# One reciprocal of a product in place of two reciprocals: products moved to GpSimd in a fused attention and neighbour kernel

## The reference, cut to what matters

```python
idx = _knn(x_loc, 30)                       # top 30 of 1024, per point
rel = pts[bidx, idx] - pts[:, :, None, :]   # xr, yr, zr
sxy2 = xr * xr + yr * yr
r2 = sxy2 + zr * zr
rho = jnp.sqrt(jnp.maximum(r2, TINY))
sxy = jnp.sqrt(jnp.maximum(sxy2, TINY))
deg_r, deg_p = r2 < TINY, sxy2 < TINY
theta = jnp.arctan2(jnp.where(deg_r, 0.0, zr), jnp.where(deg_r, 1.0, sxy))
phi = jnp.arctan2(jnp.where(deg_p, 0.0, yr), jnp.where(deg_p, 1.0, xr))
sph = jnp.stack([rho, theta, phi], axis=-1)
feat = jnp.concatenate([sph, sph - jnp.mean(sph, axis=-1, keepdims=True)], axis=-1)
# three layers of matmul, batch norm and leaky relu on feat, then a softmax over the 30
```

## Time and profile before

| what | before |
|---|---|
| median of 3 runs | 6317.76 us (6315.41 to 6318.28) |
| the profiled execution: its time, its span | 6316.55 us, 6314.8 us |
| TensorE matmul busy | 5517.6 us (87%) |
| VectorE busy | 5699.2 us (90%) |
| ScalarE busy | 4499.4 us (71%) |
| GpSimd busy | 3397.5 us (54%) |

### The profile page before, as it was taken

The page is one execution under the profiler, slowest core; times in us unless marked ns, Lnnn a source line. Parts: engine busy times, 40 slices in busy tenths (PEclk is TensorE's granted clock), DMA queues, the critical chain, the costliest instruction groups (busy, mean ns, idle before and its releaser), DMA issues. The chain is left out here.

```text
span 6314.8 us, 227176 instructions
## 1 busy us (share of the span) xinstructions
PE 5517.6 (87%) x82516; PEld 3384.3 (54%) x82516; DVE 5699.2 (90%) x8045; ACT 4499.4 (71%) x17145; POOL 3397.5 (54%) x3375
## 2 busy tenths in 40 slices
PE   7888888888888888888888888888669859999999
PEld 3555555555555555555555555555433347777776
DVE  7999999999999999999999999999855687777786
ACT  7888888888888888888888888888604623333333
POOL 3466666666666666666666666666620033333332
PEclk9999999999999999999999999999879979999999
DMA  2333333333333333333333333333340023333332
GB/s 45 95 105 97 99 98 96 95 95 107 98 110 91 99 98 96 97 97 109 96 107 93 97 97 97 97 108 92 106 108 0 0 64 89 94 87 88 84 94 74
DMA packets 651349, 568.72 MB, mean 90 GB/s; under 512 B 553072, under 2 KB 574832, under 8 KB 616208
## 3 DMA queue, kind: packets, MB, share of 16 engines
q1 hardware_dynamic: 613264, 284.51, 19.2%
q10 hardware_dynamic: 36864, 268.45, 12.0%
HBM read 384.76 MB, written 67.24 MB: 72 GB/s over the span
## 5 line engine op out<-in xcount | busy, mean ns | idle before, releaser
L722 ACT ACTIVATE prob<-SC,row_max 128x64 f32<-128x64 f32 x6144 | 1842.2, 337 | 389.7 <-DVE row_max L1046 381.6
L835 POOL TENSOR_TENSOR prob<-prob,row_rec 128x512 f32<-128x512 f32 x768 | 830.2, 1082 | 1433.5 <-DVE row_rec L1054 1403.5
L722 ACT ACTIVATION_READ_ACCUMULATOR prob<-SC,row_max 128x1 f32 x6144 | 1393.0, 230 | 0.0
L1038 DVE FIND_INDEX8 nbr<-top,dist 128x8 uint16<-128x1024 f32 x1024 | 1234.4, 1217 | 0.0
L1031 DVE MAX8 top<-dist 128x8 f32<-128x1024 f32 x1024 | 1190.8, 1203 | 1.7
L1033 DVE MATCH_REPLACE8 dist<-top,dist 128x1024 f32<-128x1024 f32 x768 | 923.3, 1206 | 0.0
L586 PE MATMUL SC<-k_bd,q_t 128*64 128x256 f32 x6144 | 907.1, 420 | 0.0
L1697 ACT ACTIVATE dense<-DM 128x512 f32<-128x512 f32 x512 | 305.6, 597 | 747.0 <-PE DM L1656 746.7
L607 PEld LDWEIGHTS PT<-ident,prob 128*128 128x128 f32 x3072 | 361.7, 145 | 833.8 <-issue 815.6
L1805 DVE TENSOR_TENSOR d_oh_a<-lo,iota_a 128x4096 bf16<-128x4096 bf16 x256 | 583.9, 2291 | 239.7 <-PE DM L1656 239.1
L607 PE MATMUL PT<-ident,prob 128*128 128x128 f32 x3072 | 490.9, 284 | 351.0 <-ACT prob_t L729 350.3
(11 more groups left out here) (187 smaller groups left out, 9475.7 us busy)
## 6 DMA issues: line engine op xcount, KB each, us to landing
low_all<-low_scratch ACTq DMA_DIRECT2D x256, 1024.0 KB, 5.0
k_bd<-k_t SPq DMA_DIRECT2D x3072, 16.0 KB, 1.9
placed<-compact SPq DMA_DIRECT2D x256, 192.0 KB, 3.8
ctx<-in_ctx SPq DMA_DIRECT2D x32, 512.0 KB, 6.2
mask<-in_mask SPq DMA_DIRECT2D x32, 512.0 KB, 8.7
xb<-in_x SPq DMA_DIRECT2D x32, 512.0 KB, 3.3
x_scratch<-xb SPq DMA_DIRECT2D x32, 512.0 KB, 6.9
y_scratch<-y_b SPq DMA_DIRECT2D x32, 512.0 KB, 6.6
```

Source lines behind the costliest of these rows:

```text
L722: last = act.activation(prob[:, s % 4, g * CHUNK:(g + 1) * CHUNK], SC[:, s % 2, g * CHUNK:(g + 1) * CHUNK], ACT.Exp, bias=row_max[:, s % 2 ...
L835: pool.tensor_tensor(pr, pr, row_rec[:, r % 2, :].unsqueeze(2).to_broadcast([128, 8, CHUNK]), ALU.mult).then_inc(normed, 1)
L1038: last = dve.max_index(nbr[:, uu % BPB, t, k * 8:(k + 1) * 8], best, row)
```

## The change

The two denominators are multiplied on GpSimd to one product `both` (128x256) directly behind `base`. VectorE takes the reciprocal of that product alone, half as many values. While it does, GpSimd multiplies each leg by the other angle's denominator (two instructions of 128x256 at step 43, with a wait for their end), and `ratio` becomes that cross product times the one reciprocal, read for both angles. Apart from this, the two clamps at step 36 use one operation each (`max`, `is_ge`) without the multiplication by 1.0.

```diff
 APART_AT, SQUARE_REL_AT, R2_AT, ROOT_AT, LEGS_AT, ACROSS_AT, BASE_AT, INVERSE_AT = 34, 35, 36, 38, 39, 41, 42, 43
+CROSS_AT = 43
...
-        hot, ratio, base = low_all, apart[:, 0:2, :], sqr[:, 0:2, :]
+        hot, ratio, base, both = low_all, apart[:, 0:2, :], sqr[:, 0:2, :], sqr[:, 2, :]
...
                     pool.tensor_tensor(base[:, :, :], sides[:, 1:3, :], sides[:, 2:4, :], ALU.add).then_inc(base_ready, 1)
+                    pool.wait_ge(base_ready, START + b + 1)
+                    pool.tensor_tensor(both, base[:, 0, :], base[:, 1, :], ALU.mult).then_inc(both_ready, 1)
+                v = lagging(i, s, CROSS_AT)
+                if v is not None:
+                    b = i * BPB + v
+                    for c in range(2):
+                        last = pool.tensor_tensor(ratio[:, c, :], legs[:, c, :], base[:, 1 - c, :], ALU.mult)
+                    last.then_inc(cross_ready, 1)
+                    pool.wait_ge(cross_ready, START + b + 1)
...
-                    pool.tensor_scalar(r2m[:, 0:3:2, :], r2[:, :, :], TINY, 1.0, ALU.max, ALU.mult).then_inc(r2_step, 1)
-                    pool.tensor_scalar(good[:, :, :], r2[:, :, :], TINY, 1.0, ALU.is_ge, ALU.mult).then_inc(good_ready, 1)
+                    pool.tensor_scalar(r2m[:, 0:3:2, :], r2[:, :, :], TINY, None, ALU.max).then_inc(r2_step, 1)
+                    pool.tensor_scalar(good[:, :, :], r2[:, :, :], TINY, None, ALU.is_ge).then_inc(good_ready, 1)
...
                     pool.wait_ge(inverse_ready, START + b + 1)
-                    pool.tensor_tensor(ratio[:, :, :], legs[:, :, :], base[:, :, :], ALU.mult).then_inc(ratio_ready, 1)
+                    pool.wait_ge(cross_ready, START + b + 1)
+                    pool.tensor_tensor(ratio[:, :, :], ratio[:, :, :], both.unsqueeze(1).to_broadcast([128, 2, NF]), ALU.mult).then_inc(ratio_ready, 1)
...
-                    dve.wait_ge(base_ready, START + b + 1)
-                    dve.reciprocal(base[:, :, :], base[:, :, :]).then_inc(inverse_ready, 1)
+                    dve.wait_ge(both_ready, START + b + 1)
+                    dve.reciprocal(both, both).then_inc(inverse_ready, 1)
```

More of the change, by code:

```diff
@@ L306, in attention_and_neighbours @@
         base_ready = sem("base_ready")
+        both_ready = sem("both_ready")
+        cross_ready = sem("cross_ready")
         turn_ready = sem("turn_ready")
```

## The result

| what | before | after |
|---|---|---|
| median | 6316.59 us (6311.62 to 6318.28, 4 runs) | 6276.49 us (6274.01 to 6278.85, 4 runs) |
| the profiled execution: time, span | 6316.55, 6314.8 | 6277.67, 6275.9 |
| end of stage 1; length of stage 2; of stage 3 | 4634.3; 458.0; 1222.5 | 4595.1; 456.0; 1224.8 |

The ratio is 0.9938, with an interval of 0.9921 to 0.9955: 40 us less, 44 were forecast. The stages are bounded by VectorE's first rows behind them, the settings of `L` and of `placed` to a constant. All of the gain comes out of the first, 39.2 us. From the first reciprocal behind 600 us to that of the 26th batch after it (starts in VectorE's timeline) a batch takes 141.57 us before (680.13 to 4361.07) and 140.14 after (679.79 to 4323.54): 1.43 us less per batch.

The account below looks back on a forecast made before the run. VectorE, 98% busy in the steady first stage, was taken to bound the kernel. Gains of 24 (reciprocal), 17 (compare) and 3 (drain), 44 us, took 6316.55 to 6272.5; the median stands 1.2 above, so 6274, range 6248 to 6308.

Parts of the forecast that it names:

- The reciprocal, 1.75 us: VectorE, step 43: reciprocal of 256 values takes 1.75 us, saving 1.59 us per batch.
- The arctangent 0.8 us late in the mean: ScalarE: arctangent waits 0.8 us for GpSimd's `ratio`, so 0.8 of 1.59 us remain, 24 us over 30 batches.
- All that follows on ScalarE and TensorE is later by that: Behind the arctangent: the 0.8 us lateness passes on, lengthening VectorE's wait for scores before the row maximum.
- the clock in a rival: TensorE before the scores: each added microsecond of work at half clock costs half a microsecond; rival's chance 0.20.
- I take 0.7, by the cast: GpSimd, step 36: one-operation clamps take 0.7 us, not 1936 ns; GpSimd 2.4 us sooner, step 37 compare 0.56 shorter, 17 us.
- The prediction's own sentence for that case: Step 37: with GpSimd under 1.8 us ahead, the compare meets the normalisation; nothing gained, or up to half a microsecond lost.
- VectorE's own delays between 2241 and 2258 cost nothing: VectorE, between reciprocal and the waiting row maximum: its delays are covered by its 1.45 us wait for scores.
- VectorE's other rows as before: Sign of being right: VectorE's rows other than the reciprocal and the step 37 compare keep their times.
- The drain, -3 us: Last batch's serial chain: clamps -2.4, `both` +0.8, reciprocal -1.6, cross products beside the reciprocal; 3 us gained.
- nothing is late: Rival: `ratio` is ready for the arctangent by 2244.4, all 1.59 us kept; 68 us gained, 6250; chance 0.14.
- swallowed: Rival: `ratio` late by all 1.59 us, or TensorE's idle time costs clock; 6293 to 6315; chance 0.20.
- slower: Rival: VectorE's compare runs ahead of GpSimd's `ratio`, arctangent 1.3 us later than before the change; 6337; chance 0.08.

Follow-up runs that it names:

- the final product sooner: The whole change, with `ratio` at step 44 moved directly behind the normalisation, ahead of the cast: 6267.82 us, 0.9919.
- the squares sooner: The kernel with the final product sooner, plus squared lengths, clamps and flags at step 35 instead of 36: 6279.21 us, 0.9939.
- The run without the flags: The whole change, with flags for degenerate points formed for 8 of 256 columns only, the rest set to 1 once: 6265.27 us, 0.9913.
- the filled hole: The whole change, with 12 unused identity products on TensorE ahead of the transposes at step 46: 6304.96 us, 0.9977.

## Why the prediction was right, and what in it was not

The time was forecast at 6274 and is 6276.5, the stage and the mechanism were named, and the sum still holds two errors that cancel: that the number is met this closely is luck. VectorE's own account of a batch, in means, is: reciprocal -1.60, `mask_row` +0.32, compare of step 44 +0.08, compare of step 37 -0.09, waits for scores -0.09 (1.88 to 1.79); together -1.38 of the measured -1.43. (This says where the time lies, not what caused it: a longer row ahead of a wait shortens the wait.)

- *The reciprocal, 1.75 us:* it took 1.74. Right, by the slope between the two measured forms.
- *The arctangent 0.8 us late in the mean:* it was 0.66. Right, with its cause: GpSimd's idle time was too short a cover. The run with the final product sooner took the wait away, and stage 1 ended 12 us sooner.
- *"All that follows on ScalarE and TensorE is later by that":* right on ScalarE (0.50 at the arctangent and at `prob_t`), wrong on TensorE. This is the first step that failed. VectorE's wait 21 us behind the reciprocal fell from a mean of 1.13 us to 1.06 where it was to grow; with `mask_row` and the compare (+0.40) that part of the batch became 0.34 us longer, not 0.66. So some 1.26 us of the 1.59 were kept, for 0.8 forecast: 14 us too little over 30 batches. What gave half of the lateness back lies between TensorE's transposes and its scores: over the 26 batches the transposes begin 0.65 us later (12.37 to 13.02 us behind the row maximum, in means), and the stretch from them to the scores is 0.33 us shorter (3.23 to 2.90), as the clock falls behind the transposes in most batches rather than ahead of them. The prediction had the clock in a rival, as a cost alone. Why it falls later stays open, and the lateness does not decide it: with the squares sooner, where nothing is late, the transposes had the upper level in 23 of 26 batches, with the final product sooner in 16.
- *The clamps: "I take 0.7, by the cast".* This term was mis-sized: they took 1.53 and 1.50 us, so GpSimd was ahead by 0.84 us, not 2.4. In the drain, where VectorE works on nothing beside it, a clamp took 1.49. The Trainium skill (GPSIMD Engine Reference, Performance versus the Vector engine) has 769 ns for 512 elements of a tight one-input loop, as its best case; the measured price is twice that, and decides. The prediction's own sentence for that case came true: the compare met the normalisation.

GpSimd after, step 36 to 37, and VectorE's compare, against the earlier trace rows:

```profile
2191.24 1.27 POOL L872 TENSOR_TENSOR y_b<-y_b,xb 128x512 f32<-128x512 f32 x1
2192.48 1.04 POOL L838 TENSOR_TENSOR prob<-prob,row_rec 128x512 f32<-128x512 f32 x1
```

```profile
2192.86 1.74 DVE L1098 TENSOR_SCALAR low_all<-low_all,iota_p 128x4096 bf16<-128x4096 bf16 x1
```

  The compare ends 1.1 us behind the GpSimd instruction that was running when it began, exactly as before, only that this is now the normalisation. 1.75 us in the mean for 1.84: 3 us in all, not 17. The run without the flags shows that 1.29 was to be had.
- *"VectorE's own delays between 2241 and 2258 cost nothing":* right. Each of the 26 batches still has the wait for the scores behind them, 0.68 us at the least, and the row maximum begins 0.05 us behind the scores' end as before. The longer `mask_row` (+0.32) and compare (+0.08) only shortened that wait. But *"VectorE's other rows as before"* was wrong, by these two.
- *The drain, -3 us:* the chain of the last batch, from its first difference (L937 before, L949 after) to the end of the stage, fell from 23.88 us to 22.02, 1.9. But ahead of it GpSimd waited 2.27 us for a copy of ScalarE, where it had waited 0.32:

```profile
4569.30 1.54 POOL L936 TENSOR_TENSOR picked<-picked,oh_b 128x768 f32<-128x768 f32 x1 [2.27 <-ACT picked L751]
```

  so the drain gave nothing. Why that copy came later was not followed.

Of the rivals, *nothing is late* fell with the wait of the arctangent, *swallowed* with 1.43 us kept per batch, and *slower* with the order of rows: `ratio` begins at 2228.78, the compare at 2230.01. In sum: 0.46 us per batch too little for the reciprocal, 0.47 too much for the compare, and 3 us too much for the drain.

## What to carry to other kernels

Moving arithmetic from the bound engine to one with idle time is paid in the idle time that lies between the moved result and its reader; count that stretch instruction by instruction, then look whether the reader can be served earlier by reordering (12 us here). A stretch in which TensorE waits cost twice here, by the wait and by the clock behind it, and useless products in the hole were worth their place (16 us of the first stage in the filled hole). And when an edit in one stage slows another that it does not touch, look for stops without a cause at the beginning of a loop, and shift the list of instructions by some products before dropping the edit.

## What the runs showed of the hardware that was not expected

- A clamp of 128x512 on GpSimd takes 1.93 us with two operations, 1.50 with one, also beside an idle VectorE; a cast of the same shape 0.635. One input and one pass do not set the price.
- Eight to fourteen unused products (12 take 2.84 us) ahead of the transposes hold the granted clock at 1.00 instead of 0.50 to 0.57 at the scores (with 8 in 25 of 26 batches), and take the scores from 1.97 to 1.08 us.
- The length of TensorE's list ahead of a loop moves the loop's time: by 160 or 240 instructions 43 to 46 us in 14 passes, by 256 or 280 nothing.
- VectorE and GpSimd hold each other up in certain forms: the compare at 1.26 us or 1.74 to 1.97, `mask_row` 0.46 or 0.81, `oh_b` 1.27 or 1.65, by what GpSimd runs beside them. For the compare and `oh_b` runs that move GpSimd's work show it; for `mask_row` it is read from the one batch.
